# Splitting the attention's output projection into three products of rounded parts

## The reference, cut to what matters

```python
x = x + tanh(g_xattn[0]) * expert_mix(layernorm(x), ctx)            # stage A
x = x + tanh(g_ffn[0])   * receptance_mix(layernorm(x), W_r, W_k, W_v)  # stage B
x = x + tanh(g_xattn[1]) * attention(layernorm(x), ctx)             # stage C
x = x + tanh(g_ffn[1])   * experts_top2(layernorm(x))               # stage D
# inside attention, 16 heads of 16 channels:
out = softmax(q k^T / 4) v          # attended values, (256, 256) an image
return out @ w_out + b_out          # the product that is changed
```

## Time and profile before

| what | us |
|---|---|
| three runs: median (lowest, highest) | 433.49 (430.86, 435.5) |
| the profiled execution's own time | 430.59 |
| its span, first to last instruction | 428.8 |
| busy in the span: PE / PE weight loads / DVE / ACT / POOL | 384.8 / 246.6 / 268.7 / 182.4 / 204.1 |
| mean granted TensorE clock, share of full | 0.963 |

### The profile page before, as it was taken

How to read it: one execution, slowest core, us unless ns; L and a number is a source line. 1 busy time by engine, 2 the same in 40 slices (tenths; PEclk the granted TensorE clock), 3 DMA queues, 4 the chain that set the end, 5 groups by cost and what they waited for, 6 DMA issues and landing times.

```text
span 428.8 us, 8863 instructions
## 1 busy us (share of the span) xinstructions
PE 384.8 (90%) x2446; PEld 246.6 (58%) x2447; DVE 268.7 (63%) x770; ACT 182.4 (43%) x376; POOL 204.1 (48%) x434
## 2 busy tenths in 40 slices
PE   1989999998999989989889989779999999972997
PEld 1658888874665756657555544234444444432996
DVE  3477988834565773972885887747555555551554
ACT  3566765546457446463464331212322222221231
POOL 3235677602231218515627648855544444443762
PEclk9999999999999989997999999889999999995999
DMA  7651000480220221421126333633333333217992
GB/s 220 193 153 52 0 2 0 146 338 2 100 99 17 84 100 55 151 99 52 54 68 268 108 113 110 215 121 106 113 110 112 112 112 112 99 73 256 315 348 86
DMA packets 26909, 52.30 MB, mean 122 GB/s; under 512 B 6309, under 2 KB 17626, under 8 KB 26490
## 3 DMA queue, kind: packets, MB, share of 16 engines
q1 hardware_dynamic: 21450, 36.13, 25.5%
q0 software_dynamic: 4992, 15.66, 9.6%
q10 hardware_dynamic: 432, 0.07, 0.1%
HBM read 32.99 MB, written 18.87 MB: 121 GB/s over the span
## 4 chain that ended last, share of the span: by engine, by line
PE 75%; DVE 10%; issue 4%; POOL 3%; ACT 2%; SPq 2%; DMA 2%; DVEq 0%; POOLq 0%
PE bank L1104 24%; PE bank L842 10%; PE bank L849 7%; PE bank L960 3%; DVE th L1291 3%; PE bank L974 3%; PE bank L881 2%; PE bank L836 2%; PE bank L990 2%; PE bank L872 2%; PE bank L980 2%; PE bank L918 2%; DVE mx L1283 2%; PE bank L1175 2%; PE bank L1176 2%
## 5 line engine op out<-in xcount | busy, mean ns | idle before, releaser
L1104 PE MATMUL bank<-w,aT 128*128 x312 | 144.0, 604 | 3.3 <-ACT aT L774 3.3
L1104 PEld LDWEIGHTS bank<-w,aT 128*128 128x128 f32 x312 | 57.3, 194 | 61.5 <-issue 61.5
L1512 DVE TENSOR_TENSOR kbd<-bank,b 128x512 f32<-128x512 f32 x39 | 26.9, 690 | 35.0 <-PE bank L1104 35.0
L687 ACT ACTIVATE b<-bank 77x512 f32<-77x512 f32 x64 | 32.7, 590 | 27.4 <-PE bank L960 27.4
L774 ACT ACTIVATE aT<-bank 128x256 f32<-128x256 f32 x39 | 14.9, 381 | 69.2 <-PE bank L1095 69.2
L440 POOL TENSOR_SCALAR shift<-mv 128x2 f32<-128x2 f32 x24 | 5.4, 225 | 75.5 <-DVE mv L1215 75.4
L1283 DVE TENSOR_REDUCE mx<-bank 128x4 bf16<-128x308 f32 x64 | 25.7, 464 | 24.0 <-PE bank L935 24.0
L554 POOL DMA_INDIRECT hidden_dram<-xk,numbers_u x26 | 28.4, 1091 | 10.2 <-issue 10.2
L553 POOL TENSOR_TENSOR carrier<-zeros 128x1 f32<-128x1 f32 x39 | 7.7, 198 | 45.5 <-DVE xk L1517 25.6
L620 ACT ACTIVATE z<-xres,shift,rstd 128x256 f32<-128x256 f32 x48 | 26.1, 596 | 3.0 <-POOL shift L443 3.0
L1209 DVE BATCH_NORM_STATS2 stats<-xres 128x6 f32<-128x256 f32 x64 | 23.9, 414 | 5.4 <-issue 5.0
(11 more groups left out here) (181 smaller groups left out, 856.5 us busy)
## 6 DMA issues: line engine op xcount, KB each, us to landing
w<-in_w SPq DMA_DIRECT2D x8, 1024.0 KB, 4.9
b<-hidden_dram SPq DMA_DIRECT2D x16, 512.0 KB, 5.0
z<-slots_dram SPq DMA_DIRECT2D x26, 136.0 KB, 2.1
xres<-in_x SPq DMA_DIRECT2D x8, 256.0 KB, 5.5
b<-in_b SPq DMA_DIRECT2D x1, 2048.0 KB, 8.6
b<-in_b SPq DMA_DIRECT2D x2, 1024.0 KB, 6.2
out_dram<-xr SPq DMA_DIRECT2D x8, 256.0 KB, 3.9
kbd<-slots_dram SPq DMA_DIRECT2D x13, 136.0 KB, 2.1
```

The source lines that it names most:

```text
L687: act.activation(flat(probs[:, NQ * k + j, :, :]), ring[j][0:C, :], ACT.Exp, scale=HD ** -0.5).then_inc(exp_done, 1)
L1104: ins = pe.matmul(hid[w][m][:, :], slT[w][:, kt, :], w_1[:, bass.ds(e, 1), kt, m * F:(m + 1) * F].rearrange("p e f -> p (e f)"), start=(kt ...
L1512: dve.tensor_tensor(val_h[w], hid[w][0][:, :], bias[0], ALU.add).then_inc(val_ready, 1)
```

## The change

w_out is split once, in turn 0: ScalarE writes a rounded copy `w_out_hi` (float32r), VectorE the rest `w_out_lo`. The attended values of each image are split the same way: ScalarE writes `attT_hi` (`high_part`), VectorE `attT_lo` (`low_attended`). `project` becomes twelve float32r products in place of four float32 ones. `attT` becomes single (it lives in `aTs[0]`), and the four new buffers share the memory of w_r, w_k, w_v and `aTs[1]`, which are free after stage B. In the ScalarE list `high_part(m)` stands between `transposed3(m-1)` and `transposed` of image m+2; in the VectorE list `low_attended(m)` stands after `moments` and before `take_logits(m-1)`.

```diff
--- before.py
+++ after.py
@@ -119,7 +119,13 @@
         def sems(name, count):
             return [sem(f"{name}{k}") for k in range(count)]
 
-        w_r, w_k, w_v, w_q, w_out = (sb(n, [P, KT, D]) for n in ("w_r", "w_k", "w_v", "w_q", "w_out"))
+        until_attention = ExitStack()
+        w_r, w_k, w_v, aTs1 = (until_attention.enter_context(nc.sbuf_tensor(n, [P, KT, w], F32)) for n, w in (
+            ("w_r", D), ("w_k", D), ("w_v", D), ("aTs1", T + 1)))
+        until_attention.close()
+        w_out_lo, w_out_hi, attT_hi, attT_lo = (sb(n, [P, KT, w], F32R)[:, :, 0:D] for n, w in (
+            ("w_out_lo", D), ("w_out_hi", D), ("attT_hi", T), ("attT_lo", T + 1)))
+        w_q, w_out = (sb(n, [P, KT, D]) for n in ("w_q", "w_out"))
         w_kv = sb("w_kv", [P, KT, 2 * D])
         w_g = sb("w_g", [P, KT, E])
         w_o = sb("w_o", [P, FT, D])
@@ -151,7 +157,7 @@
         cx = [sb(f"cx{k}", [C, D]) for k in range(CXB)]
         cxT = sb("cxT", [P, B, KT, C])
         aT = pair(sb, "aT", [P, KT, T])
-        aTs = pair(sb, "aTs", [P, KT, T + 1])
+        aTs = [sb("aTs0", [P, KT, T + 1]), aTs1]
         kT = pair(sb, "kT", [P, KT, C])
         vbd = pair(sb, "vbd", [C, H, QR])
         xr = pair(sb, "xr", [P, KT, T])
@@ -227,7 +233,7 @@
         ka = [flat(kaz[u][:, :, :])[:, 0:KT * T].rearrange("p (k t) -> p k t", k=KT) for u in range(2)]
         z3 = [z3own[0], z3own[1], kaz[0], kaz[1]]
         qT, zc = xk, xr
-        attT = [aTs[u][:, :, 1:T + 1] for u in range(2)]
+        attT = aTs[0][:, :, 1:T + 1]
         num = flat(th[0][:, :, :]).rearrange("p (k t) -> p k t", k=KT)
         rden = flat(th[1][:, :, :])[:, 0:T]
 
@@ -274,6 +280,8 @@
             "q_ps", "q16_ready", "q_ready", "v_ps", "v_ready", "s_ps", "max_done", "mT_ps", "mT_ready"))
         st_ps, exp_done, den_ps, pv_done, rden_ready, num_ready, spread_ps, attT_ready, out_ps = (sem(n) for n in (
             "st_ps", "exp_done", "den_ps", "pv_done", "rden_ready", "num_ready", "spread_ps", "attT_ready", "out_ps"))
+        attT_hi_ready, attT_lo_ready, w_out_hi_ready, w_out_lo_ready = (sem(n) for n in (
+            "attT_hi_ready", "attT_lo_ready", "w_out_hi_ready", "w_out_lo_ready"))
         bout_done, x3_done, var3_ready, rstd3_ready, z3_ready, z3T_ps, aT3_ready, lg_ps, lg_taken = (sem(n) for n in (
             "bout_done", "x3_done", "var3_ready", "rstd3_ready", "z3_ready", "z3T_ps", "aT3_ready", "lg_ps", "lg_taken"))
         dl_ready, el_ready, oh_ready, rank_ps, rank_taken, slot_ready, weights_ready = (sem(n) for n in (
@@ -707,6 +715,16 @@
                 after(act, attT_ready, n)
                 after(act, x2_done, B)
                 act.activation(num, halves(nums), ACT.Copy).then_inc(num_ready, 1)
+
+            def output_weights():
+                act.wait_ge(kk_ps, B)
+                act.activation(w_out_hi, w_out[:, :, :], ACT.Copy).then_inc(w_out_hi_ready, 1)
+
+            def high_part(n):
+                after(act, attT_ready, n + 1)
+                after(act, y_ps, B)
+                after(act, out_ps, n)
+                act.activation(attT_hi, attT, ACT.Copy).then_inc(attT_hi_ready, 1)
 
             def transposed3(n):
                 after(act, z3T_ps, n + 1)
@@ -764,6 +782,10 @@
                     numerators(m)
                 if image(m - 1) and image(m):
                     transposed3(m - 1)
+                if m == 0:
+                    output_weights()
+                if image(m):
+                    high_part(m)
                 if image(m + 2):
                     transposed(2 * B + m + 2)
                 if image(m + 1):
@@ -991,8 +1013,20 @@
                 ins.then_inc(spread_ps, 1)
 
             def project(n):
-                after(pe, attT_ready, n + 1)
-                by_token(halves(gen[0]), attT[n % 2], w_out).then_inc(out_ps, 1)
+                after(pe, w_out_lo_ready, 1)
+                dst = halves(gen[0])
+                for t in range(TT):
+                    of = slice(t * P, (t + 1) * P)
+                    if t == 0:
+                        after(pe, attT_hi_ready, n + 1)
+                    for kt in range(KT):
+                        pe.matmul(dst[:, t, :], attT_hi[:, kt, of], w_out_hi[:, kt, :], start=(kt == 0), stop=False)
+                        pe.matmul(dst[:, t, :], attT_hi[:, kt, of], w_out_lo[:, kt, :], start=False, stop=False)
+                    if t == 0:
+                        after(pe, attT_lo_ready, n + 1)
+                    for kt in range(KT):
+                        ins = pe.matmul(dst[:, t, :], attT_lo[:, kt, of], w_out_hi[:, kt, :], start=False, stop=(kt == KT - 1))
+                ins.then_inc(out_ps, 1)
 
             def transpose3(n):
                 after(pe, z3_ready, n + 1)
@@ -1294,7 +1328,12 @@
                 after(dve, spread_ps, n + 1)
                 after(dve, num_ready, n + 1)
                 after(dve, out_ps, n - 1)
-                dve.tensor_tensor(attT[n % 2], num, halves(gen[0]), ALU.mult).then_inc(attT_ready, 1)
+                dve.tensor_tensor(attT, num, halves(gen[0]), ALU.mult).then_inc(attT_ready, 1)
+
+            def low_attended(n):
+                dve.wait_ge(attT_hi_ready, n + 1)
+                after(dve, out_ps, n)
+                dve.tensor_tensor(attT_lo, attT, attT_hi, ALU.subtract).then_inc(attT_lo_ready, 1)
 
             def added(n):
                 after(dve, out_ps, n + 1)
@@ -1491,6 +1530,12 @@
                         weights(p)
                 if m > -3 and image(m + 3):
                     moments(2 * B + m + 3)
+                if m == 0:
+                    dve.wait_ge(w_out_hi_ready, 1)
+                    dve.wait_ge(r_ps, B)
+                    dve.tensor_tensor(w_out_lo, w_out[:, :, :], w_out_hi, ALU.subtract).then_inc(w_out_lo_ready, 1)
+                if image(m):
+                    low_attended(m)
                 if image(m - 1) and image(m):
                     take_logits(m - 1)
                 if m == 4:
```

## The result

The changed kernel takes 441.36 us (median of 4 runs, 439.56 to 442.61); the kernel before, run beside it, 434.5 (4 runs, 430.86 to 437.43). The ratio is 1.0225, 95% interval 1.017 to 1.028: slower by 2.2%, where 0.7% was forecast, and 1.4 us above the range. The profiled execution took 439.56, its span is 437.7 and its mean granted clock 0.944, against 0.963.

A forecast was written before the change was run, and what follows sets the result against it. It took ScalarE's exponentials to hide the projection in ordinary turns, PE following ScalarE's copies at turn ends. Added waits 0.90 + 0.3 + 1.33 + 0.44 = 2.97 us gave 436.5 us (+0.7%), range 433.0 to 440.0.

The forecast's parts named there:

- The clock falls once or twice more; slower: Added PE idle in turn 0 or before turn 7's ranks lowers PE's clock: 438.2 to 439.9 us, chance 0.27.
- Turn 0, +0.90: In turn 0 high_part delays ScalarE's transposed, so PE's maxima and everything behind it come 0.90 us later.
- Turns 1, 2, 4, +0.1 each: At these turns' ends high_part pushes transposed back: +0.1 us each, 0.3 together.
- Turns 3 and 5, 0: High_part costs nothing there, since transposed waits for PE's transposes, late by the low clock.
- Turn 6, +1.33: Low_attended waits for high_part, delaying take_logits and a VectorE chain without a gap up to added: ranks 1.33 us later.
- PE idle before the ranks, "0.65 to about 2": In turn 7 the change raises PE's idle time before the ranks from 0.65 to about 2 us.
- Last projection, +0.44: After turn 7 PE waits for high_part, then 0.2 us for low_attended: +0.44 us, saving included.
- Saving of PE, 0.29 a projection and hidden: Twelve products take 1.44 us instead of 1.73; in turns 1 to 6 the exponentials hide the saving.
- Rival 2: PE is the bound and the projection saving counts: 2.3 us faster, 431.2 us, chance 0.06.
- Rival 3: Turn 6's VectorE delay is absorbed, perhaps the last projection's too: +1.7 us, 435.2 us, chance 0.16.
- rival 4: The twelve products run as slowly as the old ones: +3.4 us a projection, 28 us if unhidden, chance 0.01.
- Its own signs of being wrong: Ordinary turns shorter by 0.3, ranks moved under 1 us against turn 6's attended, or changed low-clock total between 92 and 228.

The follow-up runs named there:

- third group: Runs on one chip beside the kernel before (mean 433.4 us): a_same2, a_fill0, b_fill0 and moved, testing unused PE products in turn 0 and moved splits.
- a_same: Changed kernel run again without any edit: 445.17 us, ratio 1.019 to the kernel before.
- a_same2: Changed kernel run again without any edit, on another chip: 439.95 us, ratio 1.016 to the kernel before.
- b_same: Kernel before, run again without any edit: 442.79 us, ratio 1.010 to itself.
- a_fill0: Changed kernel with extra unused PE products in turn 0 only (three and two): 436.66 us, ratio 1.009 to the kernel before.
- b_best: Kernel before with unused PE products in its waits as in b_fill, but four instead of one ahead of the ranks: 427.28 us, ratio 0.989.
- b_fill: Kernel before with unused PE products in the waits of turns 0, 3, 5, 6, 7, one ahead of the ranks: 428.98 us, ratio 0.998.
- split_fill: Changed kernel with both splits but the old float32 projection, plus unused PE products in its waits: 430.82 us, ratio 0.991 to the kernel before.
- prod_fill: Changed kernel with twelve products but attended values not split (times only), plus unused PE products in its waits: 427.27 us, ratio 0.984 to before.
- a_fill: Changed kernel with the unused PE products of b_fill, but five ahead of the ranks: 430.04 us, ratio 0.998 to the kernel before.
- first group: Runs on one chip: kernel before and changed kernel unedited again, and each half of the change alone; kernel before beside them 440.2 us mean.
- b_fill0: Kernel before with extra unused PE products in turn 0 only: 430.95 us, ratio 0.996 to the kernel before.
- a_fill7: Changed kernel with five unused PE products ahead of the ranks of turn 7 only: 439.98 us, ratio 1.017 to the kernel before.
- b_fill35: Kernel before with unused PE products in turns 3 and 5 only, four each: 433.65 us, ratio 0.996 to the kernel before.
- moved: Changed kernel with splits moved to idle places, last projection left float32 and unsplit, no extra products: 434.87 us, ratio 1.007 to the kernel before.
- moved_fill: The kernel moved with unused PE products in its waits, two ahead of the ranks: 428.13 us, ratio 0.993 to the kernel before.
- moved_best: The kernel moved_fill with four instead of two unused PE products ahead of the ranks: 427.09 us, ratio 0.989 to the kernel before.

## Why the prediction was wrong

**The failed step is the clock.** The sum has only the waits, 2.97 us; it puts the change in low time at nothing, with no other reason than that "one such fall already lies in turn 6, and a shifted phase can as well lose one". The prediction gave the clock its own case, "*The clock falls once or twice more; slower*", with chance 0.27 and "+1.7 each, up to +3.4". The runs put the changed kernel's low time 7.8 us above before (44.1 to 36.3, third group), that is more than two of its falls of 3.4, and in nearly every execution: of the changed kernel's 14 (result, a_same, a_same2) one has 36 us or less, of the kernel before's 111 in the five groups 50 (though b_same, the same program, has none of 4, and its mean of 47.4 us is no less than a_same's 46.6). What such a microsecond costs can be read in three ways: 2.5 us for 8.0 (a_same2 to a_fill0), 6.7 for 22.8 (before to b_best), 3.2 for 7.0 (turn 5 of before against turn 5 of b_fill); 0.3 to 0.45 us. It is under the half that pure PE work would lose; my reading, argued and not tested alone, is that PE's waits take part of it in. So 7.8 us are 2.3 to 3.5, and with the 3.0 of waits the sum is 5.3 to 6.5, where 6.3 was measured in that group (439.7 - 433.4) and 6.9 in the medians of the result. Without low time in the attention, what is left is the waits: 3.2 us between split_fill and prod_fill. The case was right in kind, with too little low time and too low a chance. Its 1.7 us for 3.4 of low time is more than the 1.0 to 1.5 that the three readings give, and the fall of turn 0, 13.8 us of low time, cost 4.0 in one piece (19.74 against a_fill's 15.74).

The prediction also took the wrong lesson from the one profile of before. It counted that execution's falls as the kernel's, and set the rival against them. It also misplaced them: the windows of before have falls in turns 3, 5 and 7 (0.91, 0.83, 0.89) and none in turn 6 (1.00). But the clock is no constant of a kernel: the same program came out with 34 to 55 us of low time within the first group. The Trainium skill (TensorE: Matmul & The Clock Gate, What's actually happening) says that "the default state is throttled, and activity releases the throttle"; the filling products, which do nothing but keep PE active, agree: low time 40.4 to 17.6 us.

Not shown is which place carries the changed kernel's extra low time. The wait before the ranks of turn 7 (2.49 us in the changed kernel, 2.02 in b_fill0 at full clock) does have a fall behind it in the changed kernel's profile, but not in b_fill0's, and a_fill7 gave nothing back. Turn 0 falls in both kernels, before the change has run anything, and not more often with the change. There is one profile for each kernel, and it would take the profiles of many executions.

**Point by point.**

- *Turn 0, +0.90:* +0.97 with filling products, +1.13 without. Right.
- *Turns 1, 2, 4, +0.1 each:* 15.84 against 15.71 to 15.78. Right.
- *Turns 3 and 5, 0:* +0.12 each at full clock. The cover named (PE's transposes late by a low clock) existed only with the fall; without it these turns behave as the ordinary ones do there (15.84 in a_fill against 15.77 and 15.78 in b_fill).
- *Turn 6, +1.33:* read too high. take_logits starts 1.40 behind attended's end (215.56 to 216.96), where it started 0.06 ahead of it: +1.46. But from there to added it took 5.97 us instead of 6.51, so the ranks came 0.97 late against turn 6's start (+0.49 on PE in turn 6, then 7.14 us from turn 7's start to the ranks, 216.64 to 223.78, against 6.66 in b_fill0, both at full clock). The chain that was said to have no gap had 0.5 us to give, and one instruction holds it. Before:

```profile
212.43 0.73 DVE L1322 TENSOR_TENSOR dl<-lg,top 128x32 f32<-128x32 f32 x1
211.82 1.28 POOL L478 TENSOR_TENSOR xres<-xres,rows 128x512 f32<-128x512 f32 x1
```

  and in the changed kernel:

```profile
217.56 0.19 DVE L1361 TENSOR_TENSOR dl<-lg,top 128x32 f32<-128x32 f32 x1
215.20 1.27 POOL L486 TENSOR_TENSOR xres<-xres,rows 128x512 f32<-128x512 f32 x1
```

  The same small VectorE subtraction took 0.73 us where GpSimd's addition of 128x512 ran beside it, and 0.19 where that had ended. In nine profiles (before, b_fill, b_fill0, b_fill35, prod_fill, moved, moved_fill, b_best, moved_best) it takes 0.42 to 0.73 and ends 0.05 to 0.07 us behind GpSimd's end; in the other eleven GpSimd is done first, and it takes 0.19. The later start of take_logits took it out of that meeting, which paid 0.54 of the 1.46. "PE's own +0.48" was right to 0.01.
- *PE idle before the ranks, "0.65 to about 2":* 2.49. The 0.65 was itself a product of the low clock in that execution (0.75 over the 6.71 us ahead of the ranks); b_fill0 has 2.02 there at full clock:

```profile
221.12 0.17 PE L1025 MATMUL bank<-chosen,tri_ones 128*128 128x8 bf16 x1 [2.02 <-issue]
```

- *Last projection, +0.44:* +0.66: from the first spread to stage D 4.38 us in a_fill against 3.72 in b_fill0. The twelve products took 1.75 of it with their wait for attT_lo, not 1.64.
- *Saving of PE, 0.29 a projection and hidden:* hidden, yes; 0.11 where it can be seen, the first product alone having 0.23. Rival 2 is out: prod_fill's ordinary turns are no shorter.
- *Sum 2.97:* 2.60 in the turns of split_fill against prod_fill, which is without the last projection's wait, where 0.90 + 0.3 + 1.33 = 2.53 were predicted; 3.2 in their means. Right in size, in part because errors cancel: turn 6 was read 0.4 too high, the last projection 0.2 too low and turns 3 and 5 together 0.2 too low. Rival 3 (absorbed, 1.7) is out with it, rival 4 by the spacing of the products.
- *Its own signs of being wrong:* two came. PE's start of the ranks moved by 0.92 against turn 6's attended (7.98 to 8.90), under the 1 us named, and the low time of the attention went from about 14 to about 31 us.

The last projection, timeline of PE, a_fill:

```profile
224.07 0.35 PE L1024 MATMUL bank<-w_out_hi,attT_hi 128*128 128x256 f32 x1 [0.47 <-ACT attT_hi L727]
224.71 0.50 PE L1029 MATMUL bank<-w_out_hi,attT_lo 128*128 128x256 f32 x2
...
225.82 1.98 PE L1150 MATMUL bank<-w,aT 128*128 x4
```

## What to carry to other kernels

A saving on one engine that lies under another's work is worth nothing, and here the splits that buy it load those other engines: find their idle places first (moved), or leave the products alone. In this kernel, where PE waits about 2 us in some turns, a change with 3 us of waits cost 6.3, and filling products in the waits that were there already gave back more (6.7 us) than the change was ever to bring (2.3). Compare kernels with their low time beside the time, since the same program differed from itself by 1%.

## What the hardware showed that was not expected

- The low stretches in turns 3 and 5, where no product fills them, are 3.4 or 6.6 to 7.0 us long in all 11 profiles, with turns of 19.0 or 20.7 us. In turn 0 they are 10 to 14 us.
- A fall can cost less than half its length: turn 0 was 19.74 instead of 15.74 us long with 13.8 us of low time, 0.29 us for each.
- The first group's chip had stalls of 2 us and more in turns 4 and 6 in all four profiles, ScalarE's idle time ended by "remote"; no profile of another group has it. The kernel before took 440.2 us there in the mean, against 433.2 to 434.9 elsewhere.
- A VectorE operation on 128x32 elements took 0.42 to 0.73 us instead of 0.19 where it met a GpSimd addition of 128x512, and ended 0.05 to 0.07 us behind it, in nine profiles of nine.
